# A macaron transformer block on one core: third buffers for the probabilities, and an order of each engine's work by the slot's place in the batch

## What is computed

```python
x = x + 0.5 * ffn(layernorm(x))
x = x + attention(layernorm(x))
x = x + 0.5 * ffn(layernorm(x))

# ffn: three weights of 256 x 1024, each made ternary (-1, 0, 1 times the mean of |W|)
hidden = silu(x @ up) * (x @ gate);   out = hidden @ down
# attention: 16 heads of 16, rotary positions on q and k, causal mask
scores = q @ k.T / 4 + causal;   out = softmax(scores) @ v @ wo
```

## Time and profile before

| | us |
|---|---|
| median of 3 runs | 716.58 |
| lowest and highest | 716.39, 716.74 |
| the profiled execution: its own time | 718.6 |
| the profiled execution: span of its trace | 716.7 |
| busy in the span: PE, ACT, DVE, POOL | 608.3, 592.4, 573.9, 542.8 |
| mean granted clock of PE, as a share of 2.4 GHz | 0.95 |

### The profile page before, as it was taken

One profiled execution on the slowest core, in us unless ns is written; L12 is line 12 of the kernel. 1 busy time (PEld: TensorE's weight loads), 2 busy tenths in 40 slices (PEclk: granted clock), 3 DMA queues, 4 the chain that ended last, 5 costly groups with the idle time before them and its releaser, 6 DMA issues. The chain is left out here.

```text
span 716.7 us, 16950 instructions
## 1 busy us (share of the span) xinstructions
PE 608.3 (85%) x5961; PEld 476.3 (66%) x5961; DVE 573.9 (80%) x1448; ACT 592.4 (83%) x1179; POOL 542.8 (76%) x581
## 2 busy tenths in 40 slices
PE   1679858789999999999999999999999787878586
PEld 1367626567777787868787877777778565556365
DVE  2977566878989999998989898989898777776653
ACT  4256578889999999999999999999999878888742
POOL 3246576879898998989898989797989867675632
PEclk9999978999999999999999999999999788897889
DMA  8501467775757675758585857676775778786700
GB/s 329 185 25 30 60 113 131 126 140 117 159 115 140 116 163 101 164 99 178 104 168 96 166 111 148 131 130 132 133 148 119 163 111 148 129 141 119 129 1 30
DMA packets 311573, 90.43 MB, mean 126 GB/s; under 512 B 301761, under 2 KB 310209, under 8 KB 311489
## 3 DMA queue, kind: packets, MB, share of 16 engines
q1 hardware_dynamic: 310624, 87.06, 61.8%
q10 hardware_dynamic: 864, 2.29, 0.9%
HBM read 9.63 MB, written 4.19 MB: 19 GB/s over the span
## 5 line engine op out<-in xcount | busy, mean ns | idle before, releaser
L686 ACT ACTIVATE prob<-score_ps,exp_bias,exp_scale 128x128 f32<-128x128 f32 (+1 forms) x512 | 224.4, 513 | 15.8 <-DVE exp_bias L944 14.7
L1087 POOL TENSOR_TENSOR prob_hl<-prob,prob_hl 128x768 f16<-128x768 f32 x128 | 211.0, 1648 | 20.3 <-ACT prob_hl L697 20.3
L1092 POOL TENSOR_TENSOR hid_l<-hid,hid_h 128x512 f16<-128x512 f32 x128 | 149.3, 1166 | 91.9 <-ACT hid_h L706 91.1
L414 PE MATMUL down_ps<-tern_down,hid_h 128*128 128x256 f16 x512 | 120.1, 275 | 18.1 <-POOL hid_l L1092 16.1
L414 PE MATMUL down_ps<-tern_down,hid_l 128*128 128x256 f16 x512 | 119.9, 274 | 0.0
L697 ACT ACTIVATE prob_hl<-prob 128x768 f16<-128x768 f32 x128 | 107.9, 843 | 9.0 <-DMA raw_w<-prob_hl 8.4
L706 ACT ACTIVATE hid_h<-hid 128x512 f16<-128x512 f32 x128 | 81.2, 635 | 38.9 <-DVE hid L980 38.8
L971 DVE SCALAR_TENSOR_TENSOR silu_b<-tanh_b,up_ps 128x512 f32<-128x512 f32 x128 | 87.1, 681 | 24.8 <-ACT tanh_b L701 24.6
L701 ACT ACTIVATE tanh_b<-up_ps,tanh_scale 128x512 f32<-128x512 f32 x128 | 87.7, 685 | 21.5 <-PE up_ps L414 21.2
L980 DVE SCALAR_TENSOR_TENSOR hid<-silu_b,gate_ps 128x512 f32<-128x512 f32 x128 | 88.0, 687 | 17.0
L422 PE MATMUL score_ps<-mask_b,ident_b 128*128 128x256 bf16 x256 | 73.3, 287 | 26.9 <-ACT prob L686 26.6
(11 more groups left out here) (106 smaller groups left out, 1359.2 us busy)
## 6 DMA issues: line engine op xcount, KB each, us to landing
xs<-x SPq DMA_DIRECT2D x16, 256.0 KB, 2.8
out<-xs SPq DMA_DIRECT2D x16, 256.0 KB, 2.8
raw_w<-prob_hl SPq DMA_TRANSPOSE x128, 3.7
raw_up<-w_up_t ACTq DMA_DIRECT2D x1, 512.0 KB, 5.1
raw_up<-w_up_t SPq DMA_DIRECT2D x1, 512.0 KB, 6.8
raw_gate<-w_gate_t ACTq DMA_DIRECT2D x1, 512.0 KB, 7.3
raw_gate<-w_gate_t SPq DMA_DIRECT2D x1, 512.0 KB, 8.9
raw_down<-w_down_t ACTq DMA_DIRECT2D x1, 512.0 KB, 9.9
```

The source lines that it names most:

```text
L414: mm = pe.matmul(dst, lhs, rhs, start=flags and n == 0, stop=n == len(pairs) - 1, skip_group_check=True)
L686: e = act.activation(prob[:, n % 2, at + j * width:at + (j + 1) * width], score_ps[:, n % 2 if tile else 2, j * width:(j + 1) * width], AC ...
L1087: pool.tensor_tensor(prob_hl[:, n % 2, 1, :], prob[:, n % 2, :], prob_hl[:, n % 2, 0, :], ALU.subtract).then_inc(prob_l_done, 1)
L1092: pool.tensor_tensor(hid_l[:, n % 2, :, :].rearrange("p m n -> p (m n)"), hid[:, n % 2, :], hid_h[:, n % 2, :, :].rearrange("p m n -> p (m ...
```

## The change

1. `AHEAD` is 5: the first part of the fifth batch is done in slots 0 to 3, and slots 94 to 97 have no round any more. All else of the plan stays.
2. `prob`, `prob_hl` and `prob_t` have three buffers (`PT_BUFS` is 3). The third ones lie on `raw_down` and `raw_gate`, weights that are not read any more by then. The three waits above reach back three pairs.
3. For slots from 0 on each engine's order depends on g % 8, eight orders for PE, ACT, DVE and POOL each (the last `else` is never reached). The order for slots below 0 is another too. SP stores a result before it turns, and not after.
4. norm3 stands at place "a" of its slot; steps of the norms and of the set-up move by some slots.
5. In five steps the wait that comes last in time is now written first.

```diff
-AHEAD = 4
+AHEAD = 5
-PT_BUFS = 2
+PT_BUFS = 3
-SUM_UP_AT = FIRST_FFN - 4
-SUM_GATE_AT = FIRST_FFN - 3
+SUM_UP_AT = FIRST_FFN - 3
+SUM_GATE_AT = FIRST_FFN + 0
-CASTS_AT = FIRST_FFN + 8
-PE_DOWN_AT = FIRST_FFN + 0
+CASTS_AT = FIRST_FFN + 9
+PE_DOWN_AT = FIRST_FFN + 1
...
-            ("attn_t", 10, "b"), ("out_proj", 11, "b"), ("norm3", 13, "b")]
+            ("attn_t", 10, "b"), ("out_proj", 11, "b"), ("norm3", 13, "a")]
...
-    1: {"stats": 4, "mean": 4, "var": 8, "power": 4, "shift": 4, "apply": 3},
-    2: {"stats": 3, "mean": 3, "var": 0, "power": 3, "shift": 3, "apply": 1},
-    3: {"stats": 1, "mean": 1, "var": 20, "power": 2, "shift": 2, "apply": 1},
+    1: {"stats": 4, "mean": 4, "var": 6, "power": 4, "shift": 3, "apply": 3},
+    2: {"stats": 3, "mean": 3, "var": 24, "power": 3, "shift": 2, "apply": 1},
+    3: {"stats": 2, "mean": 1, "var": 26, "power": 2, "shift": 2, "apply": 1},
-ROPE_ADD = {-7: 0, -5: 1}
+ROPE_ADD = {-7: 0, -6: 1}
...
+        prob = [prob_2[:, 0, :], prob_2[:, 1, :], raw_down[:, 0:6 * P]]
+        prob_hl = [prob_hl_2[:, 0, :, :], prob_hl_2[:, 1, :, :],
+                   raw_gate_16[:, 0:12 * P].rearrange("p (a k) -> p a k", a=2)]
+        prob_t = [part.rearrange("p (a c q) -> p a c q", a=2, c=6) for part in
+                  (raw_w_16[:, 0:12 * P], raw_w_16[:, 12 * P:24 * P], raw_gate_16[:, 12 * P:24 * P])]
...
             def slot(g):
+                if g in FFN_ADD:
+                    store(*FFN_ADD[g])
                 for n in pair_of(g, 1):
                     turn_probs(n)
                 for b, tile in events(g, ROW_LO):
                     turn_rows(b, tile)
-                if g in FFN_ADD:
-                    store(*FFN_ADD[g])
...
-                if n >= 2:
-                    act.wait_ge(prob_l_done, n - 1)
+                if n >= PT_BUFS:
+                    act.wait_ge(prob_l_done, n - PT_BUFS + 1)
...
-                if n >= 2:
-                    act.wait_ge(prob_turned[(n - 2) % PT_BUFS], 16 * ((n - 2) // PT_BUFS + 1))
+                if n >= PT_BUFS:
+                    act.wait_ge(prob_turned[n % PT_BUFS], 16 * (n // PT_BUFS))
...
             def hidden(n):
+                dve.wait_ge(silu_done, n + 1)
+                dve.wait_ge(gate_done, n + 1)
                 if n >= 2:
                     dve.wait_ge(hid_l_done, n - 1)
-                dve.wait_ge(gate_done, n + 1)
-                dve.wait_ge(silu_done, n + 1)
```

More of the change, by code:

```diff
@@ L549, in slot @@
                 if g < 0:
+                    for name, b in uses_of(g, "a"):
+                        misc(name, b)
+                    for n in pair_of(g, 3):
+                        product_v(n)
+                    for r in round_of(g, 0):
+                        up(*r)
+                    for n in pair_of(g, 0):
+                        scores_1(n)
+                    for r in round_of(g, 0):
+                        gate(*r)
+                    for name, b in uses_of(g, "b"):
+                        misc(name, b)
+                    for r in round_of(g, 1):
+                        down(*r)
+                    for n in pair_of(g, 0):
+                        scores_0(n)
+                elif g % SLOTS == 0:
+                    for name, b in uses_of(g, "a"):
+                        misc(name, b)
+                    for n in pair_of(g, 0):
+                        scores_0(n)
+                    for r in round_of(g, 0):
+                        up(*r)
+                    for n in pair_of(g, 0):
+                        scores_1(n)
+                    for n in pair_of(g, 3):
+                        product_v(n)
+                    for r in round_of(g, 0):
+                        gate(*r)
+                    for name, b in uses_of(g, "b"):
+                        misc(name, b)
+                    for r in round_of(g, 1):
+                        down(*r)
+                elif g % SLOTS == 1:
+                    for n in pair_of(g, 0):
+                        scores_0(n)
+                    for n in pair_of(g, 0):
+                        scores_1(n)
+                    for r in round_of(g, 0):
+                        up(*r)
                     for n in pair_of(g, 3):
@@ L578, in slot @@
                         gate(*r)
+                    for r in round_of(g, 1):
+                        down(*r)
+                    for name, b in uses_of(g, "b"):
+                        misc(name, b)
+                elif g % SLOTS == 3:
+                    for r in round_of(g, 0):
+                        up(*r)
+                    for n in pair_of(g, 0):
+                        scores_1(n)
+                    for n in pair_of(g, 3):
+                        product_v(n)
+                    for name, b in uses_of(g, "a"):
+                        misc(name, b)
+                    for n in pair_of(g, 0):
+                        scores_0(n)
+                    for r in round_of(g, 0):
+                        gate(*r)
                     for name, b in uses_of(g, "b"):
@@ L717, in slot @@
                 if g < 0:
+                    for name, b in uses_of(g, "a"):
+                        misc(name, b)
                     for b, tile in events(g, ROPE_HI):
                         rope_hi(b, tile)
-                    for name, b in uses_of(g, "a"):
-                        misc(name, b)
+                    for n in pair_of(g, 0):
+                        exps(n, 0)
                     for n in round_numbers(g, 0):
@@ L733, in slot @@
                         exps(n, 1)
-                    for n in pair_of(g, 1):
-                        prob_hi(n)
-                else:
+                    for b, tile in events(g, ROPE_HI):
+                        rope_hi(b, tile)
+                    for n in round_numbers(g, 0):
+                        hidden_hi(n)
+                elif g % SLOTS == 2:
                     for name, b in uses_of(g, "a"):
@@ L754, in slot @@
                         hidden_hi(n)
+                else:
+                    for name, b in uses_of(g, "a"):
+                        misc(name, b)
+                    for n in pair_of(g, 0):
+                        exps(n, 1)
+                    for b, tile in events(g, ROPE_HI):
+                        rope_hi(b, tile)
+                    for n in round_numbers(g, 0):
+                        hidden_hi(n)
+                    for k, b in norms(g, "apply"):
+                        norm_apply(k, b)
+                    for n in round_numbers(g, 0):
+                        tanh(n)
+                    for n in pair_of(g, 0):
+                        exps(n, 0)
+                    for name, b in uses_of(g, "b"):
+                        misc(name, b)
+                    for n in pair_of(g, 1):
+                        prob_hi(n)
             def tanh_scale_there():
@@ L911, in misc @@
                         dve.wait_ge(rope_loaded, 32)
+                    dve.wait_ge(misc_written, through(name, b))
                     if b:
                         dve.wait_ge(rope_done, 2 * b + tile - 1)
-                    dve.wait_ge(misc_written, through(name, b))
                     dve.tensor_tensor(rope_c[:, tile, :], misc_ps[:, :], cos[:, tile, :], ALU.mult)
```

633 lines of the change are left out of this document (579 added, 54 removed).

## The result

The change takes 692.73 us (median of 4 runs, 691.84 to 692.81), the kernel before 716.49 in the same session (4 runs, 715.99 to 716.74). The ratio is 0.9666, 95% interval 0.965 to 0.9683. Forecast were 701.1 us and a gain of 15.5; it became 23.8. The profiled execution took 692.75 us with a span of 690.9.

What follows compares the result with a forecast made beforehand. Four engines nearly full in the middle, ACT most; latency bounds the half-filled batches. Terms 0 + 1.0 - 1.3 - 9.0 - 1.5 - 1.2 - 3.5 + 0 = -15.5 took 716.6 to 701.1 us; own range 696 to 706, 8-in-10 range 690 to 713.

Steps and rivals of the forecast that it cites:

- rival C: ACT's whole idle time in the middle and its whole wait for transposes go: 691.4 us; chance 0.15.
- The even middle: Nine full batches, 165.0 to 503.8 us: new orders free ACT's waits, -1.0 a batch, -9.0 in all (-15.9 to +6).
- the knot at norm3: Slot 1 of 8: norm3's round through PSUM's spare bank idles PE 1.05 us, 8.0 in all; the new order removes it.
- Waits turned round: DVE's "hidden" waits for silu first, in 128 rounds: taken as 0, at most 2.9 us slower.
- AHEAD 5: Four rounds move from slots 94 to 97 to slots 0 to 3: +1.0 there, -1.5 where they leave.
- rival D: Rounds of slots 98 to 101 run at half clock, so 503.8 to 577.2 gains nothing: 702.6 us; chance 0.05.
- The order of half-filled batches: New order gives -1.3 in the batch from 128.7 and -1.2 in the two from 503.8 to 577.2.
- Third buffers: From 577.2 to 675.7 us, ACT's waits for transposes shrink while PE still waits: -3.5 (-8 to +2).
- The rest: SP's earlier store, set-up (-1.5 to +2) and norm3 of the last batch (-2 to +2): 0.
- B: Waits change places: orders free only -3.0 instead of -9.0, third buffers -1.0 instead of -3.5: 709.6 us; chance 0.21.
- E: Slower: ACT waits long for norm3's transposes in slot 1 of 8; 723.6 us at 2.0 a batch; chance 0.07.
- F: Nothing: gains and new waits cancel within 0.2%, 716.6 us; chance 0.04.

Runs made afterwards that it cites:

- experiment 10: The change with the old order on all four engines in slots with g % 8 == 1, norm3 back at place "b": 702.79 us, ratio 0.9802.
- experiment 9: The kernel before with four kinds of wait order at DVE's `hidden`, rotating over the rounds: 714.37 us in one run.
- experiment 1: The kernel before with only the five steps' waits turned, the last-answered written first: 711.36 us, ratio 0.9898.
- experiments 8 and 12: Two runs of the change with AHEAD 4 instead of 5: 692.63 us, ratio 0.9648, and 691.63 us, ratio 0.9639.
- experiment 11: The change with AHEAD 4 and waits turned in four more steps on PE, DVE and ACT: 693.77 us, ratio 0.9653.
- Experiment 4: The change with AHEAD 4 and PT_BUFS 2, keeping orders, leads and turned waits: 697.36 us, ratio 0.9705.
- Experiments 2: The kernel before with third buffers alone (PT_BUFS 3 and the three waits of the change): 715.48 us, ratio 0.9974.
- Experiment 7: The change without third buffers (PT_BUFS 2), AHEAD 5 kept: 695.68 us, ratio 0.9694.

## Why the prediction was right, and where its sizes were off

The change is faster, and by the cause that was named for the largest term. That the time lies in the range is owed to the range's width: it was drawn to take in rival C, and the gain is 8.3 us larger than forecast. By parts:

**The even middle: -9.0 forecast, -10.4 measured. Right, and for the reason given.** The largest cause was the knot at norm3: experiment 10 puts 6.0 of the 10.4 on that slot's order, and PE's wait at the knot is what came back with it. The slot's other steps moved along on all four engines, so the share of the knot alone is argued. Two details were wrong. The new wait of ACT for norm3's transposes (0.5) isn't there: I had ACT ready for the copy 0.09 us after the transposes begin (351.31 and 351.22), and in the change it is ready 0.59 us after (309.82 and 309.23), 0.05 us ahead of their end, since the new orders shift the whole slot and not only the copy. And part of the middle's gain belongs to a term that I had at nothing, below.

**Waits turned round: 0 forecast, -7 alone.** Here the step failed, in its sign. I wrote that "the gap must hold the end of silu whichever way the waits stand", bounded the term by 0 and +2.9, and took the 0.12 us in the earlier trace rows for the least there could be. The rows could not show that most of it hangs on the waits' order. The gap went to 0.03 (0.81 to 0.71 from start to start), and experiment 9 shows that it is the waits' order and nothing else. DVE's idle time ahead of hidden fell from 17.0 in the page before to 2.9. In the old order the five steps are worth 7 us and hidden alone about 5, also in the middle (338.8 to 335.5 in experiment 1), where I had thought DVE's 31 us of idle time would cover it. They don't cover it. I take it that an engine's idle time covers nothing on a chain that others wait for (here tanh, silu, hidden and its rounding, from ACT to DVE and back); that was not tried apart. In the new order the medians say 2.4 us, not clear of noise; the middle's 1.2 is in step with it. The Trainium skill ("VectorE: DVE Perf Modes", The DRAIN you can't avoid) has it that a semaphore between two VectorE operations costs nothing extra. The traces here do not bear that out, in any order of the waits. With the blocking wait first, hidden starts 0.71 us after silu's start; an operation that needs nothing of hidden (norm3's low part, L898) starts 0.61 after hidden's, with 0.68 and 0.69 us for the operations ahead. With two waits ahead of the blocking one experiment 9 measured 0.10 us more still.

**AHEAD 5: +1.0 and -1.5 forecast; +3.1 and about -4 measured.** The sum, about nothing, was nearly right, by two misses against each other. Four rounds are not worth the 1.5 us that I took from the difference of full and half-filled batches. Between experiments 8 and 12 and the change, first batch: 33.7 to 36.8; pairs 88 to 104: 69.6 (mean of the two) to 65.6. From 104 to 127 it is 90.0 to 92.3, but experiment 11 has 92.9 there with AHEAD 4, so that is not shown to come from AHEAD. The difference I took the price from compared an old full batch with half-filled ones that were themselves late for another reason, their order. In the new order three to four of the 5.3 us of ACT's work count, about three times what I had taken. The granted clock did what was foretold: from 92.3 to 105 it was 0.70 before, over the change's first slots it is 1.00, and the batch got no shorter (36.4 and 36.8). What the clock gave back is inside AHEAD's +3.1 and can't be told apart from it. The two stretches, of before and of the change, and the change's lowest one at the hole of slots 94 to 97:

```profile
92.30:105.00 12.70, 6.65 (x42) 2.82 (x42) 7.19 (x23) 10.45 (x22) 10.49 (x13) 0.70 0.64 131
```
```profile
93.60:105.00 11.40, 9.71 (x85) 7.10 (x84) 8.95 (x22) 10.65 (x24) 10.88 (x14) 1.00 0.58 104
...
522.00:527.00 5.00, 3.99 (x28) 1.99 (x25) 3.22 (x12) 3.51 (x8) 2.53 (x3) 0.79 0.57 108
```

The new low stretch came where it was foretold, but it is short, and from 526.8 to 558.7, where the rounds of 98 to 101 run, the clock is 1.00. So rival D's mechanism isn't there.

**The order of half-filled batches: -1.3 and -1.2 forecast, the largest miss.** Experiment 4 has the orders and turned waits without the other two parts: -3.2 in the first batch, -1.9 in the second, -3.7 from 88 to 104 and -5.0 from 104 to 127. I had no term at all for the order in the first batch and none from pair 104 on. That the first batch came out at +0.4 where I had +1.0 is luck: AHEAD's +3.1 and the order's -3.2 cancel. I had said that these batches are bound by latency; then a shorter chain from engine to engine is worth more there than in a full batch, and I should have given each of them at least the 1.0 of a full one.

**Third buffers: -3.5 forecast, about -2.** Experiments 2 and 7 give 1.9 and 2.0, neither clear of noise by itself. The mechanism was as argued, and stronger: ACT's wait for the transpose is gone, PE's is still there (from about 500 us to the end 9.2 before, 10.2 in the change), and in the old order pairs 104 to 127 gained nothing. (Of the 6.3 us of ACT that I halved, 5.7 lie in the stretch to which I gave the term.) Experiment 7 puts the gain in the new order at 1.9 in those pairs, against the 3.5 of the forecast. The rest of the -6.3 I put down to the order, which alone gave 5.0 there. What I did not see is that the parts depend on each other: with AHEAD 4 the third buffers are worth 4 to 5 us (0.9705 in experiment 4 against 0.9648 and 0.9639 in 8 and 12), nearly all of it in the middle (331.8 against 327.8 and 328.1), where ACT waits 2.9 us for transposes with two of them. With AHEAD 5 and two buffers that wait is 0.2 us. Why was not tried.

**The rest: 0.** Set-up and the last stretch gave +1.3 and -1.1, within the bounds. Whether the store ahead of the transposes plays a part was not tried.

**The rivals.** C (all idle time goes) has the right time from the wrong place: ACT kept 6.1 us of idle time in the middle (98.1% busy and a batch of 36.5, as foretold for the forecast), and the end gave more than C has there. B and E are refuted by the middle, F by the time. Of E's mechanism, ACT waiting for norm3's transposes, 6.7 us remain, five times and all behind 493 us. The longest (2.4, at 654.55) follows a product with v that itself waited 2.2 us for its transpose, as E had it:

```profile
ACT raw_up L784 <- PE misc_ps L512: 6.7, 5, 2.4
...
ACT prob L824 <- DVE exp_bias L1233: 5.0, 8, 0.8
```

What stays open is how the other 0.45 us of a full batch's gain divide over the seven other orders and the waits.

## What to carry to other kernels

Write the wait that will be answered last first: on VectorE each wait ahead of it cost 0.04 to 0.06 us per operation, and in the old order this added up to 1% of the kernel without an operation moved. Look for the one place where a shared buffer's round (here a bank of PSUM: transposes, copy, low part) makes the busiest producer stand, and take that slot's order first; one slot's order in eight carried 10 of 24 us. Where batches are half empty, the present length of a batch underprices a piece of work that is moved: four rounds came out at 3.1 and 4 us, between the 1.5 of that reading and the 5.3 of the busiest engine's work. Expect a better order to give more there than in full batches. And measure parts of a change together as well as apart: the third buffers were worth 2 us with one plan of rounds and 4 to 5 with the other.

## What was not expected of the hardware

The start of a VectorE operation depends on the order in which its waits are written. In this kernel `hidden`, behind the operation that it needs, starts 0.71 us after that one's start with the blocking wait first, 0.77 with one wait ahead and 0.81 with two; one wait or two behind the blocking one made no difference that shows. On ScalarE the same was read twice in experiment 11, 0.07 to 0.08 us of gap with one wait ahead and 0.03 with none. Turning such waits on PE, ACT and DVE too gave nothing that could be measured in the whole kernel.
